# Attention values with unpadded stationary tiles: one 128-column matmul per head pair, head blocks masked behind PSUM, low part of y on GpSimd

## The reference, cut to what matters

```python
qkv = (x @ W_qkv.T).reshape(B, L, 3, H, dk)        # B = L = 64, D = 256, H = dk = 16
q, k, v = (qkv[:, :, 0], qkv[:, :, 1], qkv[:, :, 2])
k = _layernorm(k)
gamma = jax.nn.sigmoid(log_gamma).reshape(1, H, 1, 1)
def step(S, qkv_t):
    q_t, k_t, v_t = qkv_t
    S = gamma * S + v_t[..., :, None] * k_t[..., None, :]
    y_t = jnp.einsum('bhde,bhe->bhd', S, q_t)
    return (S, y_t)
...
return y @ W_o.T
```

## Time and profile before

| | us |
|---|---|
| device time, median of 3 runs | 284.82 (284.54 to 285.0) |
| span of the profiled execution, first to last instruction | 282.7 |
| PE busy in it | 268.2 (95%) |
| DVE busy | 235.1 (83%) |
| ACT busy | 166.6 (59%) |
| POOL busy | 144.5 (51%) |

### The profile page before, as it was taken

The page is one execution under the profiler, slowest core; times in us unless marked ns, Lnnn a source line. Parts: engine busy times, 40 slices in busy tenths (PEclk is TensorE's granted clock), DMA queues, the critical chain, the costliest instruction groups (busy, mean ns, idle before and its releaser), DMA issues.

```text
span 282.7 us, 10701 instructions
## 1 busy us (share of the span) xinstructions
PE 268.2 (95%) x4692; PEld 194.3 (69%) x4699; DVE 235.1 (83%) x489; ACT 166.6 (59%) x276; POOL 144.5 (51%) x138
## 2 busy tenths in 40 slices
PE   5988999989999999999999999999999999998995
PEld 5857779668878878888977977987864434433331
DVE  7999998599699796776777965867888999999995
ACT  2773465445567454355236156234599999857991
POOL 6939594880791394386188033003004668860561
PEclk9999999999999999999999999999999999999999
DMA  5980404402600800710530220130005920000167
GB/s 184 322 255 2 151 2 160 144 5 50 252 5 3 297 6 2 242 60 5 191 112 5 77 78 5 30 123 5 3 2 188 381 81 20 0 1 0 59 252 288
DMA packets 19279, 28.59 MB, mean 101 GB/s; under 512 B 1888, under 2 KB 9632, under 8 KB 19232
## 3 DMA queue, kind: packets, MB, share of 16 engines
q1 hardware_dynamic: 19232, 27.90, 29.1%
HBM read 19.48 MB, written 8.42 MB: 99 GB/s over the span
## 4 chain that ended last, share of the span: by engine, by line
PE 71%; DVE 19%; ACT 4%; issue 3%; DMA 1%; POOL 1%; DVEq 0%; ACTq 0%
PE psum L813 16%; PE psum L1229 9%; PE psum L854 7%; PE psum L838 6%; PE psum L876 5%; PE psum L1248 3%; PE psum L918 3%; PE psum L994 2%; ACT silu L776 2%; PE psum L1000 2%; PE psum L1001 2%; PE psum L897 2%; PE psum L998 2%; PE psum L996 2%; PE psum L995 2%
## 5 line engine op out<-in xcount | busy, mean ns | idle before, releaser
L1423 DVE TENSOR_TENSOR arena<-psum,xq_mem 128x512 f32<-128x512 f32 x64 | 39.7, 683 | 9.4 <-PE psum L838 9.4
L477 POOL TENSOR_TENSOR xT_lo<-arena,xT 128x512 fp32r<-128x512 f32 x14 | 18.0, 1306 | 46.3 <-ACT xT L618 46.3
L1229 PE MATMUL psum<-xq_mem,guT 128*128 128x512 bf16 x149 | 33.7, 379 | 0.4 <-issue 0.2
L603 ACT ACTIVATE arena<-psum,pmask 128x512 f32<-128x512 f32 x32 | 20.1, 684 | 15.8 <-PE psum L1001 15.8
L1229 PEld LDWEIGHTS psum<-xq_mem,guT 128*128 128x128 bf16 x152 | 14.4, 98 | 19.4 <-DVE arena L1625 1.8
L854 PEld LDWEIGHTS psum<-arena 64*32 64x32 f32 x2048 | 21.8, 105 | 7.1 <-issue 6.7
L854 PE MATMUL psum<-arena 64*32 64x64 f32 x2048 | 25.9, 225 | 0.5 <-DVE arena L1423 0.4
L618 ACT ACTIVATE xT<-arena 128x512 fp32r<-128x512 f32 x14 | 8.1, 622 | 30.5 <-PE psum L813 25.9
L1636 DVE TENSOR_REDUCE h_max<-arena 128x1 f32<-128x1024 f32 (+1 forms) x24 | 25.9, 1122 | 0.2
L758 ACT ACTIVATE silu<-psum,gu_x 128x1024 f32<-128x1024 f32 (+1 forms) x24 | 24.5, 1029 | 2.1 <-PE psum L1229 1.1
L838 PE MATMUL psum<-arena 32*64 32x128 f32 x1024 | 19.3, 278 | 1.1 <-issue 1.1
(11 more groups left out here) (255 smaller groups left out, 738.0 us busy)
## 6 DMA issues: line engine op xcount, KB each, us to landing
arena<-in_x SPq DMA_DIRECT2D x9, 512.0 KB, 4.0
x_dram<-arena SPq DMA_DIRECT2D x8, 512.0 KB, 3.5
pooled<-x_dram SPq DMA_DIRECT2D x8, 512.0 KB, 5.0
out<-pooled SPq DMA_DIRECT2D x15, 256.0 KB, 2.1
xin<-in_x_t SPq DMA_DIRECT2D x7, 512.0 KB, 4.8
cs_rows<-cs_dram SPq DMA_DIRECT2D x12, 256.0 KB, 5.1
pooled<-in_w_qkv_t SPq DMA_DIRECT2D x3, 256.0 KB, 4.5
pooled<-in_w_down SPq DMA_DIRECT2D x1, 704.0 KB, 7.6
```

The source lines that it names most:

```text
L477: pool.tensor_tensor(xT_lo[:, k, :], xrotT[:, k, :], xT[:, k, :].bitcast(F32), ALU.subtract).then_inc(xl_ok, 1)
L603: act.activation(qblk[:, c, odd, :], Q_BANK[c][:, :], ACT.Identity, scale=pmask[:, odd:odd + 1]).then_inc(q_ok, 1)
L1229: mm = pe.matmul(o[:, 512 * half:512 * half + 512], gT[i][:, c, v * P:v * P + P], xq[:, c, TB * n + 512 * half:TB * n + 512 * half + 512], ...
L1423: dve.tensor_tensor(dec[:, c, r, :, :], bank[S_BANK[r]].rearrange("q (n k) -> q n k", n=PP), two_heads, ALU.mult).then_inc(dec_done, 1)
```

## The change

`vpad` goes; v is kept in plain rows (`v_rows`). Per head pair and sequence there is one matmul of 128 columns: both heads' v times both heads' scores. Of its output the blocks even-even and odd-odd are wanted and the cross blocks are not. ACT takes the even columns out of PSUM with a row mask (`y_even`), DVE adds the odd columns with the other row mask (`y_odd`) into `y_sum`, ACT rounds `y_sum` to `yT` (`y_high`), and POOL subtracts (`low_y`). In the last group `hidden_of_y` reads `y_sum`, and the copies to `y_all` go. `weights_turn` goes ahead of `hidden_of_y` there.

```diff
@@ gpsimd
+            def low_y(g, half):
+                for b in range(2):
+                    pool.wait_ge(yT_ok, 4 * g + 2 * half + b + 1)
+                    pool.tensor_tensor(y_part(yT_lo, b, half), y_sum[:, half, b], y_part(yT, b, half).bitcast(F32), ALU.subtract).then_inc(yl_ok, 1)
             for g in range(G):
                 if g + 1 < G:
                     low_x(g + 1)
                 if g + 2 < G:
                     rotate(g + 2)
-                allowed(g)
+                low_y(g, 0)
+                if g + 1 < G:
+                    allowed(g)
+                low_y(g, 1)
+            allowed(G - 1)
@@ scalar
-            def y_copy(g, half):
+            def y_even(g, half):
                 act.wait_ge(y_mm, 2 * g + half + 1)
...
                 for b in range(2):
-                    act.activation(y_part(yT, b, half), y_psum(b, half), ACT.Copy).then_inc(yT_ok, 1)
+                    act.activation(y_rows(b, half), y_psum(b, half, 0), ACT.Identity, scale=pmask[:, 0:1]).then_inc(ye_ok, 1)
+            def y_high(g, half):
+                for b in range(2):
+                    act.wait_ge(y_ok, 4 * g + 2 * half + b + 1)
+                    act.activation(y_part(yT, b, half), y_sum[:, half, b], ACT.Copy).then_inc(yT_ok, 1)
@@ tensor, values
-                at_y = (c * 2 + i) * S
-                for odd in range(2):
-                    for b in range(2):
-                        rows = slice(S * b, S * b + S)
-                        for r in range(QR):
-                            at_v = (c * QR + r) * 64 + odd * 32
-                            last = pe.matmul(Y_BANK[half][b][32 * r:32 * r + 32, at_y:at_y + S], vpad[rows, p, at_v:at_v + 32],
-                                             dec[rows, c, r, p, odd * S:odd * S + S], start=(odd == 0), stop=(odd == 1))
+                at_y = (c * 2 + i) * P
+                for b in range(2):
+                    rows = slice(S * b, S * b + S)
+                    for r in range(QR):
+                        at_v = (c * QR + r) * 32
+                        last = pe.matmul(Y_BANK[half][b][32 * r:32 * r + 32, at_y:at_y + P], v_rows[rows, p, at_v:at_v + 32],
+                                         dec[rows, c, r, p, :], start=True, stop=True)
@@ vector
-            dve.memset(vpad, 0.0).then_inc(zeros, 1)
...
-            def low_y(g, half):
-                if g == G - 1:
...
-                    dve.tensor_tensor(y_part(yT_lo, b, half), y_psum(b, half), y_part(yT, b, half).bitcast(F32), ALU.subtract).then_inc(yl_ok, 1)
+            def y_odd(g, half):
+                for b in range(2):
+                    dve.wait_ge(ye_ok, 4 * g + 2 * half + b + 1)
+                    dve.scalar_tensor_tensor(y_rows(b, half), y_psum(b, half, 1), pmask[:, 1:2], y_rows(b, half), ALU.mult, ALU.add).then_inc(y_ok, 1)
```

More of the change, by code:

```diff
@@ L82, in build @@
         qblk = carve(DC * 2 * TG).rearrange("p (c h t) -> p c h t", c=DC, h=2)
-        vpad = carve(PP * 512).rearrange("p (n k) -> p n k", n=PP)
+        v_rows = carve(PP * D).rearrange("p (n k) -> p n k", n=PP)
         dec = carve(DC * QR * 512).rearrange("p (c r n k) -> p c r n k", c=DC, r=QR, n=PP)
@@ L212, in build @@
         base_ok = sem("base_ok")
-        zeros = sem("zeros")
         kinds_f = sem("kinds_f")
@@ L285, in pool_rows, with y_psum, y_rows @@
             return y[:, :, TG * c:TG * c + TG].rearrange("q k (p b j) -> q b k p j", b=2, j=S)
-        def y_psum(b, half):
-            return Y_BANK[half][b][:, 0:D].rearrange("q (c n t) -> q c n t", c=DC, n=2)
+        def y_psum(b, half, odd):
+            return Y_BANK[half][b].rearrange("q (c n o t) -> q o (c n) t", c=DC, n=2, o=2)[:, odd]
+        def y_rows(b, half):
+            return y_sum[:, half, b].rearrange("q c n t -> q (c n) t")
         def y_part(y, b, half):
@@ L700, in _ @@
                         k_copies(g + 1, 1)
-                y_copy(g, 0)
+                y_even(g, 0)
+                if g == 0:
+                    k_copies(g + 1, 1)
+                y_high(g, 0)
                 if g + 1 < G:
-                    if g == 0:
-                        k_copies(g + 1, 1)
                     q_copies(g + 1, 0)
-                y_copy(g, 1)
+                y_even(g, 1)
+                y_high(g, 1)
                 if g == G - 1:
@@ L929, in hidden_weights, with halves @@
                 last.then_inc(w1o_mm, 1)
-            def halves(k, w, tokens_of, start=False, stop=False):
+            def halves(w, tokens_of, start=False, stop=False):
                 for h in range(2):
-                    last = pe.matmul(w1_bank(G - 1)[NA * h:NA * h + NA, 0:TG // 2], w, tokens_of[:, k, TG // 2 * h:TG // 2 * (h + 1)],
-                                     start=start, stop=stop)
+                    last = pe.matmul(w1_bank(G - 1)[NA * h:NA * h + NA, 0:TG // 2], w, tokens_of(h), start=start, stop=stop)
                 return last
@@ L940, in hidden_of_x @@
                 for k in range(DC):
-                    halves(k, w1_sb[:, k, :], xinT, start=(k == 0))
+                    halves(w1_sb[:, k, :], lambda h: xinT[:, k, TG // 2 * h:TG // 2 * (h + 1)], start=(k == 0))
             def hidden_of_y():
-                pe.wait_ge(y_act, 2)
-                pe.wait_ge(y_dve, 2)
+                pe.wait_ge(y_ok, 4 * G)
                 for k in range(DC):
-                    last = halves(k, w1o[:, k * NA:k * NA + NA], y_all, stop=(k == DC - 1))
+                    last = halves(w1o[:, k * NA:k * NA + NA], lambda h: y_sum[:, h, :, k].rearrange("q b n t -> q n b t"), stop=(k == DC - 1))
                 last.then_inc(w1_mm, 1)
@@ L1553, in _ @@
                 if g == G - 1:
-                    low_y(g, 0)
+                    y_odd(g, 0)
                 if g:
@@ L1569, in _ @@
                     link(dve.reciprocal(clip_s[:, 2, :], clip_s[:, 1, :]))
-                low_y(g, 1)
+                y_odd(g, 1)
                 if g == 0:
```

24 lines of the change are left out of this document (8 added, 16 removed).

## The result

| | before | after |
|---|---|---|
| device time, median | 284.77 (4 runs, 284.54 to 285.0) | 301.48 (4 runs, 299.36 to 303.15) |
| span of the profiled execution | 282.7 | 301.4 |
| its granted TensorE clock, mean | 1.000 | 0.966 |

The change costs 5.9%: the ratio is 1.059, with a 95% interval of 1.0555 to 1.0624. The forecast of 292.7 (289.5 to 296) had the direction and was 8.8 us too short, outside its own range.

The account below looks back on a forecast made before the run. PE was taken to bound the kernel before, at 22.86 us a group. Adding 4.8 us (group 0), 2.6 (groups 1 to 6) and 0.45 (group 7), 7.9 in all, took 284.82 to 292.7, range 289.5 to 296.

Parts of the forecast that it names:

- Rival 4: DVE's odd part: port contention makes it 1.02 us, adding 3.6 us in groups 1, 2 and 6, 296.3; chance 0.05.
- Group 0, T(1) = 48.5: Start of scores(1, 0) on PE, T(1), becomes 48.5, 4.8 us late, as PE waits for POOL's low parts.
- the 1.1 us from the low products to the next scores: On PE, the time from the low products of project(g, 2) to the next group's scores: 1.1 us.
- Rival 5: PE stands still twice in group 0; clock falls to 1.2 GHz for group 1's scores and values: 295.0; chance 0.05.
- Rounds: Groups 1 to 6, from T(1) to T(7): predicted 139.75 us, 2.6 us more than before.
- the path of 6.5: Each group from POOL's first pair: pair 1.3, mask 2.8, pair 1.3, PE 1.1, together 6.5 us.
- the route of the loads: To POOL's first pair: x1_done at T+0.8, the loads' landing, then 8.0 us of rotation.
- the second part of y: Group 2: the second y_odd is delayed by long weight scales, so the second pair starts at T+20.6.
- The lower end of the range: Landing of 7.03 everywhere gives back 1.5 us in groups 3 to 5, pairs of 1.2 another 1.2: 290.0.
- The last group, +0.45: Group 7: DVE's softmax waits for the mask behind the low part; 0.45 us remains after PE's 0.8 saved.
- Its saving is hidden in every one of these: Groups 1 to 6: PE alone would need 22.0 us a group, so its 0.83 us saving doesn't show.
- rival 1: Whole kernel: PE saves its full 6.6 us and all new waits are hidden, 278.2; chance 0.05.

Follow-up runs that it names:

- e11: Changed kernel without the low part of y, PE reading the high part twice: 282.9 us, ratio 0.9936.
- e10: Changed kernel with DVE's copy of the squares and newton(1) ahead of the up weights' scales, ACT's integers of them in group 1: 301.79 us, ratio 1.0579.
- e3: Changed kernel with idle matmuls in PE's pauses (20, 6 and 11 in group 0, 11 ahead of the last pooling): 301.0 us, ratio 1.0552.
- e5: Changed kernel with fewer idle matmuls than e3 (10, 3 and 5 in group 0, 5 before the last weights): 297.5 us, ratio 1.0469.
- e12: Changed kernel with DVE's first odd part of groups 1 to 6 ahead of the softmax's weights: 300.56 us, ratio 1.0548.
- e6: Changed kernel with only the last group's mask put ahead of its two low parts: 300.44 us, ratio 1.0536.
- e4: Kernel before with only the matmul of 128 columns, the odd heads' part of the values left out: 281.2 us, ratio 0.987.
- e9: e8 with the order of e10 on DVE and ACT: 284.0 us, ratio 0.9972.
- e1: Changed kernel with the mask behind both low parts in every group: 290.21 us, ratio 1.0196.
- e7: Changed kernel with low parts ahead of the mask in groups 0 to 5, mask ahead in 6 and 7: 287.23 us, ratio 1.0078.
- e8: e7 with group 0's low parts inside rotation 2 and DVE's copy of the squares ahead of the scales: 286.92 us, ratio 1.0059.

## Why the prediction was wrong, point by point

- **Prices of the parts.** Nearly right: values 19.7 against 19.3; pair of subtractions 1.40 to 1.44 against 1.3. The rule on shared ports ("SBUF — State Buffer" of the Trainium skill, section "Who interferes with whom") held: the 32 odd parts, one PSUM and one SBUF operand, took 0.465 to 0.485 us each, beside a busy POOL or not, and 0.475 on average in e11 too, where POOL has no subtractions. Rival 4 did not occur. The same rule's other half did: L1522, two SBUF operands, spread from 0.42 to 1.50 us, and the prediction used the rule for the added instruction alone.
- **Group 0, T(1) = 48.5.** POOL's two pairs end at 43.33 and 47.45, against 43.3 and 47.4. The step that failed is the 1.1 us from the low products to the next scores; at 1.2 GHz it was 2.0, nearly the whole miss of T(1). The wait for the copy of the squares was missed as well; it hid inside a wait that had been counted (e10).
- **Rival 5.** It had 0.05, and the fall of the clock that it describes came about, on top of the forecast. The argument against it was a clock at its upper level in every slice before; but that row says nothing of a kernel with pauses, and the forecast itself added two. Its price was too high where it stood and lacking elsewhere: it gave round 1 2.3 us more, and round 1 took 25.2 with the clock low and 24.0 and 24.2 in e3 and e5 with the clock held, against a forecast of 23.9. The last group, where the clock fell again, it did not have.
- **Rounds, 5.6 us too short.** Two steps failed. The first is the path of 6.5 from the start of POOL's first pair to T: it took 6.75 to 6.77, which is 1.6 us over six rounds. The second is when that pair starts, 4.0. The prediction took the route of the loads for groups 3 to 5 and for group 2 the second part of y. Measured, the first pair started at T+18.4 in group 1, T+17.5 to 17.7 in groups 2 to 4, behind a wait for y in each, T+17.2 in group 5 directly behind the rotation, and T+16.3 in group 6. In group 1 the clock is the reason: e3 and e5, with the clock held, start that pair at T+17.2 and T+17.1, where 17.4 was forecast. In group 4 it is DVE: before, it reached the same place at 127.90, T+15.6; after, at T+16.65, of which L1522, held 1.49 instead of 0.42, is the whole difference, since ACT's exponentials and its copies stand behind it. How much of the round that wait is worth by itself was not shown: e12 took it away and gained 0.9 us, less than runs of one kernel differ by. A part of the 5.6 is this execution's: the same order of rounds summed to 142.5 to 147.9 us in e3, e5, e6 and e10, so at least 2.7 us over the forecast of 139.75 are the forecast's own.
- **The lower end of the range.** A landing of 7.03 in groups 3 to 5 takes 2.5 us off the route of the loads and not 1.5; only y as the next route, at about T+16.4 by the rows, would leave some 1.5, and the text doesn't say so. It made no difference to the miss.
- **The last group, +0.45.** The mask's place was right, its price not: 4.7. The low part was ready at T(7)+17.9 instead of 17.2 and the mask at 20.65 instead of 20.0, so the softmax started at T(7)+20.76 against T(7)+19.23 before, 1.5 late. The slower clock is most of the remaining 3.2: L891 alone took 1.4 longer, and e5, with the clock held there, ended that stage 3.6 sooner. With the mask ahead 4.5 came back (e6).
- **The bound of PE.** "Its saving is hidden in every one of these" held for the changed kernel. Where POOL is out of the way 3.6 of 6.2 us come through (e4), which rival 1 had at 6.6.

## What to carry to other kernels

Work moved to a half-idle engine costs its place in that engine's queue, not its duration: the same 32 subtractions cost 18.6 us where half of them stood behind the mask, and 1.1 in e9, ahead of it or inside the rotation and with DVE's order changed too. Where the bounding engine gets new pauses, price the clock as part of the forecast, and look at every place with a pause. Where two routes end within a us of each other, price both, with the spread that each shows from one execution to the next, and expect little from shortening one.

## What the runs showed of the hardware

- The fall of the clock isn't decided by the lengths of the pauses alone. In e1 and e7 group 0 has the same two waits of PE, 1.33 and 1.91 (e7: 1.92) us. In e1 the clock stayed at 1.00; in e7 it fell, and T(1) came 1.3 us later. Two windows of each, e1 first:

```profile
44.00:46.00 2.00, 2.00 (x20) 2.00 (x18) 0.81 (x2) 1.97 (x3) 2.00 (x4) 1.00 0.00 0
46.00:48.00 2.00, 2.00 (x72) 1.70 (x71) 1.30 (x3) 0.14 (x1) 1.56 (x3) 1.00 0.03 8
```

```profile
44.00:46.00 2.00, 2.00 (x11) 2.00 (x11) 0.69 (x1) 1.88 (x2) 1.92 (x5) 0.50 0.03 8
46.00:48.00 2.00, 2.00 (x46) 1.87 (x46) 0.42 (x1) 0.00 (x0) 1.40 (x2) 0.70 0.00 0
```

- How long a small DVE operation takes beside POOL depends on which starts first. The two of L1473 (before: L1464) run beside the start of the rotation. From the timelines of the kernel before, of after and of e9, DVE's row and the first of POOL's rotation in each:

```profile
33.97 1.50 DVE L1464 TENSOR_SCALAR v_rep<-ones,cols_sb 64x64 f32<-64x64 f32 x2
34.13 1.28 POOL L463 TENSOR_TENSOR arena<-xin,cs_rows 128x512 f32<-128x512 f32 x1 [2.11 <-DMA cs_rows<-cs_dram]
```

```profile
34.14 1.28 POOL L465 TENSOR_TENSOR arena<-xin,cs_rows 128x512 f32<-128x512 f32 x1 [1.95 <-DMA cs_rows<-cs_dram]
```

```profile
34.35 0.53 DVE L1477 TENSOR_SCALAR v_rep<-ones,cols_sb 64x64 f32<-64x64 f32 x2
35.27 1.29 POOL L465 TENSOR_TENSOR arena<-xin,cs_rows 128x512 f32<-128x512 f32 x1 [3.66 <-DMA cs_rows<-cs_dram]
```

  With POOL idle both take 0.53. Before, one got ahead of POOL and the other ended with POOL's first operation. After, DVE's row at 34.14 and POOL's start in the same moment, and both operations together take as long as two of POOL's. In e8 they start together too and it is the same again; in the other ten traces in which the two meet, that of before among them, DVE starts 0.06 to 0.22 us ahead and one of its operations gets through. "SBUF — State Buffer" of the Trainium skill, section "Who interferes with whom", says that a copy, cast or tensor_scalar in a mode that uses both ports is blocked whole by a GpSimd instruction issued first; the trace agrees, with 1.09 us of PE's first wait from a shift of 0.16 us.
- The kernels that wait for POOL may spread more from run to run, which few runs can only suggest: four runs of the changed kernel spread over 3.8 us and eight of e7 over 3.4, where two sets of 17 runs of the kernel before spread over 3.1 and 1.6.
- Values of half as many records with twice the columns cost 274 instead of 225 ns a record: 24% less in all.
